# One counted semaphore read by three engines, or one taken down by TensorE and passed on

## The reference

```python
q, k, v = _fq_sym(q, axis=-1), _fq_sym(k, axis=-1), _fq_sym(v, axis=2)
attn = jnp.einsum('bhqd,bhkd->bhqk', q, k)
attn = jax.nn.softmax(attn.astype(jnp.float32), axis=-1)
attn = _fq_unsigned(attn, axis=-1)          # rounded to 255 levels of each row's maximum
out = jnp.einsum('bhqk,bhkd->bhqd', attn, v)
...
x = x + _L0_xattn_ref(...); x = x + _L0_ffn_ref(...)
x = x + _L1_xattn_ref(...); x = x + _L1_ffn_ref(...)
```

## Time and profile before

| | |
|---|---|
| median of 3 runs | 4755.82 us |
| the profiled execution | 4754.47 us, its span 4752.7 us |
| busy: PE, DVE, ACT, POOL | 96%, 85%, 82%, 77% of the span |
| second pass of heads 1 to 14 (2688 steps) | 963.2 to 4079.4 us of the span |
| mean granted clock of TensorE | 0.986; 1.00 in those heads |

### The profile page before, as it was taken

The page is one execution under the profiler, slowest core; times in us unless marked ns, Lnnn a source line. Parts: engine busy times, 40 slices in busy tenths (PEclk is TensorE's granted clock), DMA queues, the critical chain, the costliest instruction groups (busy, mean ns, idle before and its releaser), DMA issues. The chain is left out here.

```text
span 4752.7 us, 155422 instructions
## 1 busy us (share of the span) xinstructions
PE 4574.4 (96%) x53771; PEld 2006.1 (42%) x53771; DVE 4048.7 (85%) x7024; ACT 3897.0 (82%) x6715; POOL 3681.2 (77%) x3920
## 2 busy tenths in 40 slices
PE   7999999999999999999999999999999999888999
PEld 5666653333333333333333333333333333334655
DVE  6778888999999999999999999999999999774333
ACT  3555558999999999999999999999999999983121
POOL 5777777889888888888898989889888989762000
PEclk9999998999999999999999999999999999998999
DMA  3555651111111111111111111111111111342000
GB/s 99 153 159 161 176 148 47 31 34 34 33 31 35 31 34 32 34 35 30 33 35 35 31 34 33 34 31 35 34 31 33 34 35 30 129 165 89 0 37 8
DMA packets 222815, 269.11 MB, mean 57 GB/s; under 512 B 34366, under 2 KB 202809, under 8 KB 221289
## 3 DMA queue, kind: packets, MB, share of 16 engines
q1 hardware_dynamic: 167529, 203.57, 15.5%
q10 hardware_dynamic: 54528, 55.60, 3.9%
HBM read 174.57 MB, written 82.97 MB: 54 GB/s over the span
## 5 line engine op out<-in xcount | busy, mean ns | idle before, releaser
L1563 ACT ACTIVATE e_home<-ps_sweep,sk 125x448 f32<-125x448 f32 x6144 | 3439.8, 639 | 124.7 <-ACTq L1562 93.4
L1596 DVE TENSOR_REDUCE unit_max<-ps_sweep 128x1 f32<-128x500 f32 x5040 | 3002.9, 670 | 150.3 <-DVEq L1595 102.0
L1791 POOL TENSOR_SCALAR r<-e_home 125x896 f32<-125x896 f32 x2976 | 2776.4, 951 | 434.6 <-ACT e_home L1563 279.6
L1351 PE MATMUL ps_av<-e_home,zt 126*17 126x224 f32 x24576 | 1705.0, 353 | 0.0
L1296 PE MATMUL ps_sweep<-q,k_home 54*128 54x448 bf16 x5760 | 1659.9, 356 | 0.0
L1327 PE MATMUL ps_sweep<-k_home,q 48*128 48x500 bf16 x5040 | 1590.4, 377 | 40.3 <-PEq L1326 29.2
L1346 PE MATMUL ps_av<-r,vt 125*16 125x224 f16 x12288 | 851.8, 267 | 32.4 <-PEq L1337 11.7
L1327 PEld LDWEIGHTS ps_sweep<-k_home,q 48*128 48x128 bf16 x5040 | 370.1, 93 | 1183.4 <-issue 1150.1
L1346 PEld LDWEIGHTS ps_av<-r,vt 125*16 125x16 f16 x12288 | 299.1, 85 | 879.6 <-issue 879.4
L1351 PEld LDWEIGHTS ps_av<-e_home,zt 126*17 126x17 f32 x24576 | 626.5, 96 | 0.4
L1296 PEld LDWEIGHTS ps_sweep<-q,k_home 54*128 54x128 bf16 x5760 | 522.0, 93 | 64.6 <-issue 16.2
(11 more groups left out here) (269 smaller groups left out, 2918.1 us busy)
## 6 DMA issues: line engine op xcount, KB each, us to landing
k_rows<-krows ACTq DMA_DIRECT2D x48, 1000.0 KB, 7.2
k_home<-k_rows SPq DMA_DIRECT2D x408, 93.8 KB
k_home<-k_rows SPq DMA_DIRECT2D x120, 281.2 KB
e_home<-in_ctxT SPq DMA_DIRECT2D x48, 500.0 KB, 4.4
vr<-v_raw SPq DMA_DIRECT2D x128, 187.5 KB
cb<-in_ctxT SPq DMA_DIRECT2D x16, 1500.0 KB, 6.1
v_raw<-e_home SPq DMA_DIRECT2D x12, 1000.0 KB
v_raw<-vb SPq DMA_DIRECT2D x12, 1000.0 KB
```

Source lines behind the costliest of these rows:

```text
L1351: last = pe.matmul(psav[c:c + WIDE, lo:hi], zt[u][0:ONES_ROW + 1, i + s, :], e[(i + s) % SLOTS][0:ONES_ROW + 1, g, lo:hi], start=False, st ...
L1563: act.activation(e[i % SLOTS][0:KT, g, :], score_bank(i, g, both)[0:KT, 0:HALF], ACT.Exp, scale=sk[u][:, i:i + 1]).then_inc(e_wrote[h % 2], 1)
L1596: top = dve.tensor_reduce(unit_max[:, b, j * NPIECE + at:j * NPIECE + at + 1], ps[:, 0:SB], axis=AX.X, op=ALU.max)
L1791: pool.tensor_scalar(r[i % SLOTS][:, :, :], e[i % SLOTS][0:KT, :, :], 1.0, HALFWORD, ALU.mult, ALU.add)\
```

## The change

`e_wrote` becomes one semaphore that TensorE takes down by 1 for each exponential. For the half `g = 1` TensorE then raises a second semaphore by 1, on which the rounding engine waits: `e_ready` for GpSimd, `e_odd` for VectorE in head 15. Both of these are taken down by the engine that waits. ScalarE's three decrements per head go, and so do the counters in the arguments. No load, matmul, activation or DMA changes.

```diff
-        e_wrote = two("e_wrote")
-        PER_HEAD = 2 * STEPS
+        e_wrote = semaphore("e_wrote")
...
-            def exponentials(i, g, u, y, last):
-                n = next(written)
-                pe.wait_ge(e_wrote[n // PER_HEAD % 2], n % PER_HEAD + 1)
+            def exponentials(i, g, u, y, last, shared=False):
+                pe.wait_ge(e_wrote, 1).then_inc(e_wrote, -1)
+                if g == 1:
+                    pe.sem_inc(e_odd if shared and i % 2 else e_ready, 1)
                 if g == 1 and i == CT - 1:
                     pe.sem_inc(k2_free[u], 1)
...
-                if j == 0 and i == 2 * SLOTS and h > 0:
-                    for n in range(PER_HEAD // P):
-                        act.sem_inc(e_wrote[1 - h % 2], -P)
...
                     act.activation(e[i % SLOTS][0:KT, g, :], score_bank(i, g, both)[0:KT, 0:HALF], ACT.Exp,
-                                   scale=sk[u][:, i:i + 1]).then_inc(e_wrote[h % 2], 1)
+                                   scale=sk[u][:, i:i + 1]).then_inc(e_wrote, 1)
...
-                dve.wait_ge(e_wrote[(HEADS - 1) % 2], 2 * (j * CT + i) + 2)
+                dve.wait_ge(e_odd, 1).then_inc(e_odd, -1)
...
-                pool.wait_ge(e_wrote[step // STEPS % 2], 2 * (step % STEPS) + 2)
+                pool.wait_ge(e_ready, 1).then_inc(e_ready, -1)
```

More of the change, by code:

```diff
@@ L1 @@
-import itertools
 import math
@@ L1132, in attention @@
             semaphore(n) for n in ("fold_ready", "z_folded", "av_folded", "last_ready"))
-        e_free, r_ready, r_odd = (semaphore(n) for n in ("e_free", "r_ready", "r_odd"))
+        e_ready, e_free, r_ready, e_odd, r_odd = (
+            semaphore(n) for n in ("e_ready", "e_free", "r_ready", "e_odd", "r_odd"))
         ones_ready = semaphore("ones_ready")
@@ L1282, in pe_program @@
         def pe_program():
-            turn, written = Turn(), itertools.count()
-            def exponentials(i, g, u, y, last):
-                n = next(written)
-                pe.wait_ge(e_wrote[n // PER_HEAD % 2], n % PER_HEAD + 1)
+            turn = Turn()
+            def exponentials(i, g, u, y, last, shared=False):
+                pe.wait_ge(e_wrote, 1).then_inc(e_wrote, -1)
+                if g == 1:
+                    pe.sem_inc(e_odd if shared and i % 2 else e_ready, 1)
                 if g == 1 and i == CT - 1:
@@ L1300, in paired_exponentials @@
             def paired_exponentials(i, g, u, y, last):
-                exponentials(i, g, u, 1 - y, last)
+                exponentials(i, g, u, 1 - y, last, shared=True)
                 if g == 1 and i == CT - 1:
@@ L1549, in act_program, with scores @@
         def act_program():
-            def scores(h, j, i, u, v_used, both):
-                if j == 0 and i == 2 * SLOTS and h > 0:
-                    for n in range(PER_HEAD // P):
-                        act.sem_inc(e_wrote[1 - h % 2], -P)
+            def scores(i, u, v_used, both):
                 if i == 0:
@@ L1575, in chunk @@
                     for i in range(CT):
-                        scores(h2, j, i, u, not head_start or finished is not None, h1 is None)
+                        scores(i, u, not head_start or finished is not None, h1 is None)
                         if head_start and finished is not None and i == LAG - 2:
@@ L1584, in act_program @@
             act.wait_ge(e_free, SLOTS).then_inc(e_free, -SLOTS)
-            for n in range(PER_HEAD // P):
-                act.sem_inc(e_wrote[(HEADS - 1) % 2], -P)
             act.wait_ge(v_free[0], 1).then_inc(v_free[0], -1)
@@ L1637, in weights, with rounded @@
                 dve_done(dve.tensor_copy(keep[:, :], weight[:, ::-1]))
-            def rounded(j, i):
-                dve.wait_ge(e_wrote[(HEADS - 1) % 2], 2 * (j * CT + i) + 2)
+            def rounded(i):
+                dve.wait_ge(e_odd, 1).then_inc(e_odd, -1)
                 dve.tensor_scalar(r[i % SLOTS][:, :, :], e[i % SLOTS][0:KT, :, :], 1.0, HALFWORD, ALU.mult, ALU.add)\
@@ L1738, in chunk @@
                         if not first and i % 2 == 1:
-                            rounded(j, i)
+                            rounded(i)
                         if not first and i in WEIGHED:
@@ L1787, in pool_program, with rounded, chunk @@
         def pool_program():
-            def rounded(n, i):
-                step = n * CT + i
-                pool.wait_ge(e_wrote[step // STEPS % 2], 2 * (step % STEPS) + 2)
+            def rounded(i):
+                pool.wait_ge(e_ready, 1).then_inc(e_ready, -1)
                 pool.tensor_scalar(r[i % SLOTS][:, :, :], e[i % SLOTS][0:KT, :, :], 1.0, HALFWORD, ALU.mult, ALU.add)\
                     .then_inc(r_ready, 1)
-            def chunk(n, u, h, shared):
+            def chunk(u, h, shared):
                 for i in range(CT):
                     if not shared or i % 2 == 0:
-                        rounded(n, i)
+                        rounded(i)
                     if h is not None and i in SCALED:
@@ L1820, in pool_program @@
             for n in range(1, HEADS * NCH + 1):
-                chunk(n - 1, (n - 1) % 2, n // NCH if n < HEADS * NCH else None, n > (HEADS - 1) * NCH)
+                chunk((n - 1) % 2, n // NCH if n < HEADS * NCH else None, n > (HEADS - 1) * NCH)
             pool.wait_ge(vr_free, 1).then_inc(vr_free, -1)
```

## The result

The changed kernel takes 4919.95 us, median of 4 runs (4914.62 to 4924.87); the kernel before, 4755.47 in the same comparison. The ratio is 1.0344, 95% interval 1.0332 to 1.0356: 164 us slower. The forecast was 4888, in a range of 4800 to 4980.

The account below looks back on a forecast made before the run. TensorE's array was taken to bound steady steps at 1.11 us, then the loop through ScalarE at 1.17. Terms 202 - 85 + 12 + 3 = +132 us on the median gave 4888 us, range 4800 to 4980.

Parts of the forecast that it names:

- The price of the pair: TensorE's decrementing wait and raise ahead of the first score: 0.22 us over a carried wait, 0.15 for the second member.
- The loop: ScalarE's exponential to TensorE's scores and back: 2.34 us for two steps, above the array's 1.11 a step; +202 us.
- The far bound of 461 us: Heads 0 to 14, if every step paid 0.22 - 0.06 and nothing were shared between two steps: +461 us, not taken.
- What the stalls give back: Stalls of 0.059 us a step, 170 us in heads 0 to 14: half given back, -85 us, by choice.
- head 15: Scores in pairs with four banks; score 0.22 us later while ScalarE has the other half: +3 us, bounds 0 and 42.
- the 12 put down for the sequencer: TensorE's sequencer holds in ordinary steps; chunks' summing steps and edges cost some 0.1 us a chunk, 120 chunks: +12 us.
- rival C: Dearer: score's matmul 0.09 behind its load, +86 us, or three instructions in a row where VectorE's bank is last, +72; chance 0.15.
- The second half's wait: TensorE's new wait for g = 0, ahead of the second score, passes under the sums: zero; without cover +100 us.
- ScalarE's decrements: The 45 and three at the end go; they ran behind activations: zero, or 7 us back at TensorE's price.
- B: Rival of no change: the delays fall into existing stalls; 4756 us, or 4786 if all stalls shrink; chance 0.10.
- D: Faster rival: TensorE enters sums later, no longer meets late GpSimd, loop still fits; 4714 us; chance 0.03.
- What the profile would show: Steady steps 1.17 us, first score's load 0.26 to 0.27 behind the exponential, TensorE and ScalarE busy shares down 3 to 5 points.

Follow-up runs that it names:

- the run with two idle raises: Kernel before, with two raises of an unread spare semaphore ahead of the first score; GpSimd and VectorE still on ScalarE's count: 4910.74 us, ratio 1.0324.
- the third instruction: Kernel before, with three raises of an unread spare semaphore ahead of the first score (+1, +1, -2): 5104.93 us, ratio 1.0737.

## Why the prediction was right, point by point

**The price of the pair.** Two own instructions in a row were priced at 0.27 to the load and 0.30 to the matmul by the one place of the kernel that had them. Measured after: 0.26 and 0.29. The duration in the record, 0.051, would have given no change, and the run with two idle raises shows that it is not the price.

**The loop.** 2.34 us for two steps, 1.17 a step. Measured 1.176 in the timeline, 1.177 in the mean of places 8 to 15. The term was 202 us; measured, (1.177 - 1.105) x 2880 = 207. The mean was right, its two parts were not: steps with one piece were put at 1.07 before and steps with two at 1.11, +0.10 and +0.06. In the steady places they took 1.106 and 1.105 before and 1.179 and 1.178 after, so both lost 0.073, and that the average came out at 0.070 is in part luck. That the loop closes once in two steps is shown by the third instruction, +0.080 a steady step for 0.15. The far bound of 461 us is out.

**What the stalls give back.** This term was mis-sized. The stalls were put at 0.059 a step before, 170 us, and half of it, 85 us, was taken as given back, by choice. Measured they are 0.056 before (1.161 - 1.105, heads 0 to 14) and 0.039 after (1.216 - 1.177): 0.017 x 2880, some 50 us, under a third. This is where most of the forecast's missing 32 us are: 35 here, 5 in the loop and 5 in head 15 (8, where 3 were forecast), less the 12 put down for the sequencer, which the measured stalls already hold. 207 - 50 = 157 for heads 0 to 14. The reason given for it was half right. In places 0 and 5 the stalls moved up with the instructions, by 0.08 and 0.12. GpSimd, thought to be late by less, hears 0.35 later and not 0.22: place 16 went from 1.215 to 1.299, and to 1.208 where two instructions stand in front but GpSimd hears from ScalarE. The chain behind VectorE's bank grew too (see rival C). The 12 us for the sequencer can't be told apart from the rest of the stalls.

**What was costed at nothing.** The second half's wait: +4 us by itself, within a measurement's reach of nothing. ScalarE's decrements: not measured apart.

**The rivals.** B (the delays fall into stalls) is out by the steady step alone. C was wrong in one of its counts and, as far as the trace tells, right in the other: a score's matmul follows its load by 0.03 also while the other row group is busy (2239.63 and 2239.66, with a piece streaming since 2239.53), but where VectorE's bank comes last, its maximum's end is 0.417 ahead of the first score's load in the changed kernel (median), 0.148 before. That is +0.27, in 222 of the 2688 steps of heads 1 to 14, two a chunk; C had +0.30 in two steps a chunk. A single own instruction cost 30 us in such places and others like them. How much of the +164 lies in this chain isn't shown. The time came out 32 us over the forecast, not C's 72. D needed a pair under 0.06.

**What the profile would show.** The load's distance, the steady step and GpSimd's releaser came as told. TensorE's busy share did not: 99% in place of a fall by 3 to 5 points; ScalarE's fell by 2.7. The working that led to the time used neither.

## What to carry to other kernels

A wait that also decrements is an instruction of its own on the waiting engine's sequencer. On TensorE the load behind it started 0.06 us later here, and each further own instruction in a row (here the raise) cost 0.15 more, not the 0.05 of its record. A wait for a count was carried by the load behind it, at no such cost. Find the loop that crosses the engines and count what stands between its last signal and its next instruction: 156 us came from two instructions in that spot, 10 from the same two a few matmuls later. When you hand a signal on through a third engine, look for the consumer's worst place and not its mean load: GpSimd, busy for 89%, still cost some 20 us in two steps of 24 once TensorE's loop was short again. In the changed kernel as it is, that is hidden by the slower loop.

## What the runs showed of the hardware

A busy share can rise when an engine is slowed: TensorE went from 98% to 99% with the same matmuls, since two that had streamed side by side then came one behind the other. And the price of TensorE's own instructions was constant to a few nanoseconds: 0.051 with a carried wait, 0.114 with one own instruction in front, 0.264 with two and 0.415 with three, as the median distance from the exponential's end to the load in places 8 to 15, so 0.06 for the first and 0.15 for each further one. Runs with the same number in front agree within 0.002. Behind VectorE's maximum, where the piece's own wait stands in the chain already, the first one more cost 0.12 (0.148 to 0.268), the next two 0.15 each (0.417, 0.568), and with the piece's wait carried it was 0.056.
